# Summing four Mamba states per quarter on TensorE alone instead of halving them on VectorE first

## What is computed

```python
dA = jnp.exp(dt[..., None] * A)
dBx = dt[..., None] * Bm[:, :, None, :] * xs[..., None]
...
_, h = jax.lax.associative_scan(comb, (dA, dBx), axis=1)
y = jnp.einsum('blds,bls->bld', h, Cm) + D * xs
y = y * jax.nn.silu(z)
```

## Time and profile before

| | |
|---|---|
| median of 3 runs | 10564.35 us (10559.11 to 10570.2) |
| the profiled execution | 10562.82 us |
| its span, first to last instruction | 10560.5 us |
| PE matmul, busy | 71% |
| DVE, busy | 72% |
| ACT, busy | 56% |
| mean granted TensorE clock | 0.832 |

### The profile page before, as it was taken

One profiled execution on the slowest core, in us unless ns is written; L12 is line 12 of the kernel. 1 busy time (PEld: TensorE's weight loads), 2 busy tenths in 40 slices (PEclk: granted clock), 3 DMA queues, 4 the chain that ended last, 5 costly groups with the idle time before them and its releaser, 6 DMA issues. The chain is left out here.

```text
span 10560.5 us, 133751 instructions
## 1 busy us (share of the span) xinstructions
PE 7453.7 (71%) x40708; PEld 4281.7 (41%) x40708; DVE 7621.4 (72%) x10135; ACT 5890.6 (56%) x12843; POOL 796.9 (8%) x657
## 2 busy tenths in 40 slices
PE   6766666677777777777777777777777777777442
PEld 3434334444444444444444444444444444444221
DVE  3777777777777777777778777877777777777625
ACT  5555545556655665556555655565556555655211
POOL 0131313100000000000000000000000000000173
PEclk8878788888888888888888888888888888888655
DMA  3222222222222222222222222222222222222334
GB/s 125 92 84 85 92 77 100 84 94 104 95 91 94 104 98 91 91 104 102 88 91 107 100 91 92 102 99 91 99 95 100 97 95 93 105 91 86 102 60 124
DMA packets 284018, 1007.89 MB, mean 95 GB/s; under 512 B 45448, under 2 KB 135404, under 8 KB 275052
## 3 DMA queue, kind: packets, MB, share of 16 engines
q1 hardware_dynamic: 248556, 981.23, 25.7%
q0 software_dynamic: 34816, 21.19, 1.4%
HBM read 938.66 MB, written 63.58 MB: 95 GB/s over the span
## 5 line engine op out<-in xcount | busy, mean ns | idle before, releaser
L588 ACT ACTIVATE P<-psS,least_s 99x197 f32<-99x197 f32 x4096 | 1443.5, 432 | 1252.2 <-DVE least_s L759 1250.6
L1029 PE MATMUL psS<-KM,Q 128*99 128x394 f32 x4096 | 1952.3, 622 | 108.7 <-ACT PTs L594 105.7
L1036 PE MATMUL psS<-cst,P 99*99 99x99 f32 x8192 | 1227.2, 295 | 1071.2 <-ACT P L588 1048.5
L843 DVE TENSOR_TENSOR_SCAN hs<-dA,hs 128x1576 f32<-128x1576 f32 x512 | 1762.1, 3442 | 62.2
L1036 PEld LDWEIGHTS psS<-cst,P 99*99 99x99 f32 x8192 | 1034.7, 199 | 1590.8 <-ACT P L588 1383.1
L759 DVE TENSOR_REDUCE least_s<-psS 99x2 f32<-99x394 f32 x2048 | 1083.5, 561 | 611.1 <-PE psS L1029 586.2
L1029 PEld LDWEIGHTS psS<-KM,Q 128*99 128x99 f32 x4096 | 803.2, 212 | 966.4 <-issue 801.8
L664 ACT ACTIVATE dA<-dt_,aneg 128x394 f32<-128x394 f32 x2048 | 1160.9, 625 | 34.8 <-DVE hs L843 34.8
L594 ACT ACTIVATE PTs<-psS 99x396 f32<-99x396 f32 x2048 | 936.0, 531 | 430.5 <-PE psS L1036 428.8
L1119 PE MATMUL psY<-hs,cst 128*128 128x394 f32 x2048 | 897.9, 566 | 266.4 <-DVE hs L852 266.4
L834 DVE TENSOR_TENSOR hs<-hs,u 128x1576 f32<-128x1576 f32 x512 | 917.2, 1791 | 0.7 <-DMA hs<-bc_scratch 0.7
(11 more groups left out here) (186 smaller groups left out, 9778.3 us busy)
## 6 DMA issues: line engine op xcount, KB each, us to landing
hs<-bc_scratch SPq DMA_DIRECT2D x512, 788.0 KB, 4.1
cr<-bc_scratch SPq DMA_DIRECT2D x512, 788.0 KB, 5.6
pat<-patches SPq DMA_DIRECT2D x64, 1176.0 KB, 5.9
rows_scratch<-zeros SPq DMA_DIRECT2D x1, 19104.0 KB, 62.4
hs<-sum_scratch SPq DMA_DIRECT2D x24, 512.0 KB, 3.5
out<-hs SPq DMA_DIRECT2D x24, 512.0 KB, 2.6
sum_scratch<-HW SPq DMA_DIRECT2D x64, 148.5 KB
bc_scratch<-dtbc SPq DMA_DIRECT2D x128, 49.2 KB, 5.8
```

The source lines that it names most:

```text
L588: last = nc.scalar.activation(P[:, r, b, m, 0:T], psS[0:CT, 2 * r + b, m * T:(m + 1) * T], ACT.Exp, bias=least_s[:, r, b, m:m + 1], scale= ...
L843: nc.vector.tensor_tensor_scan(h, dA[:, g % 2, :, :].rearrange("p n t -> p (n t)"), h, 0.0, ALU.mult, ALU.add).then_inc(scan_ready, 1)
L1029: mm(psS[0:CT, 2 * r + b, 0:2 * T].rearrange("p (e t) -> p e t", e=2), Q[:, r, b, q * CT:(q + 1) * CT], KM[:, r, 2 * h:2 * h + 2, b, 0:T], ...
L1036: last = nc.tensor.transpose(psS[0:CT, 2 * r + b, at:at + CT], P[:, r, b, m, k * CT:(k + 1) * CT], c("ident")[0:CT, 0:CT])
```

## The change

`half` and its semaphore are gone, and PE's `sum_` waits for `mul_done` of the same quarter and issues four identity products in place of two. `UNITS` loses its eight `half` entries, and each list of `PLACE` the eight numbers that belonged to them. All other numbers stay.

```diff
@@ UNITS @@
-    UNITS += [("scan", _g)] + ([("half", _g - 1), ("sum", _g - 1)] if _g else [])
+    UNITS += [("scan", _g)] + ([("sum", _g - 1)] if _g else [])
...
-UNITS += [("half", QUARTERS - 1)]
@@ block.vector @@
-            def half(i, g):
-                dve.wait_ge(mul_done, i * MULS + MUL_OUT[g])
-                nc.vector.tensor_tensor(hs[:, g % HBUF, 0:2, :], hs[:, g % HBUF, 0:2, :], hs[:, g % HBUF, 2:4, :], ALU.add).then_inc(half_summed, 1)
@@ block.tensor, sum_ @@
-                pe.wait_ge(half_summed, i * QUARTERS + g + 1)
-                for k in range(2):
+                pe.wait_ge(mul_done, i * MULS + MUL_OUT[g])
+                for k in range(QN):
                     last = mm(psY[:, 0:N], c("ident"), hs[:, g % HBUF, k, :], start=q == 0 and k == 0, stop=False)
```

More of the change, by code:

```diff
@@ L82 @@
 STAGES = [('conv', 0), ('square', 1, 0), ('square', 0, 0), ('norm', 1, 0), ('norm', 0, 0), ('qkv', 1), ('qkv', 0), ('keys', 1, 0), ('keys', 0, 0), ('score', 1, 0, 0), ('score', 0, 0, 0), ('score', 1, 0, 1), ('score', 0, 0, 1), ('keys', 1, 1), ('keys', 0, 1), ('turn', 1, 0, 0), ('turn', 0, 0, 0), ('turn', 1, 0, 1), ('turn', 0, 0, 1), ('score', 1, 1, 0), ('score', 0, 1, 0), ('score', 1, 1, 1), ('score', 0, 1, 1), ('keys', 1, 2), ('keys', 0, 2), ('turn', 1, 1, 0), ('turn', 0, 1, 0), ('turn', 1, 1, 1), ('turn', 0, 1, 1), ('score', 1, 2, 0), ('score', 0, 2, 0), ('score', 1, 2, 1), ('score', 0, 2, 1), ('keys', 1, 3), ('turn', 1, 2, 0), ('keys', 0, 3), ('turn', 0, 2, 0), ('turn', 1, 2, 1), ('turn', 0, 2, 1), ('score', 1, 3, 0), ('score', 0, 3, 0), ('score', 1, 3, 1), ('score', 0, 3, 1), ('turn', 1, 3, 0), ('turn', 0, 3, 0), ('turn', 0, 3, 1), ('turn', 1, 3, 1), ('score', 1, 4, 0), ('score', 0, 4, 0), ('score', 1, 4, 1), ('value', 1, 0), ('score', 0, 4, 1), ('value', 0, 0), ('turn', 0, 4, 0), ('turn', 1, 4, 0), ('turn', 1, 4, 1), ('turn', 0, 4, 1), ('score', 1, 5, 0), ('score', 0, 5, 0), ('score', 1, 5, 1), ('score', 0, 5, 1), ('turn', 1, 5, 0), ('turn', 0, 5, 0), ('turn', 1, 5, 1), ('turn', 0, 5, 1), ('score', 1, 6, 0), ('score', 0, 6, 0), ('score', 1, 6, 1), ('score', 0, 6, 1), ('turn', 1, 6, 0), ('turn', 0, 6, 0), ('turn', 0, 6, 1), ('turn', 1, 6, 1), ('score', 0, 7, 0), ('score', 1, 7, 0), ('score', 1, 7, 1), ('score', 0, 7, 1), ('turn', 1, 7, 0), ('turn', 1, 7, 1), ('turn', 0, 7, 0), ('turn', 0, 7, 1), ('value', 1, 1), ('value', 0, 1), ('den', 1), ('den', 0), ('wo', 1), ('wo', 0), ('square', 1, 1), ('norm', 1, 1), ('square', 0, 1), ('norm', 0, 1), ('gate', 1), ('gate', 0), ('sig', 1), ('sig', 0), ('up', 1), ('up', 0), ('down', 1), ('down', 0), ('square', 1, 2), ('norm', 1, 2)]
-PLACE = {'dve': [0, 0, 0, 1, 3, 1, 2, 5, 8, 14, 14, 14, 15, 15, 16, 17, 19, 22, 25, 27, 27, 27, 28, 29, 30, 30, 32, 36, 38, 40, 40, 40, 41, 41, 45, 41, 42, 43, 43, 45, 47, 48, 49, 49, 49, 50, 51, 52, 52, 54, 55, 56, 57, 57, 51, 55, 59, 61, 63, 63, 64, 65, 66, 66, 66, 64, 68, 69, 72, 72, 75, 74, 75, 75, 75, 76, 77, 77, 78, 81, 82, 82, 86, 87, 89, 83, 84, 86, 88, 93, 90, 90, 90, 91, 91, 90, 92, 93, 97, 94, 95, 96, 98, 98, 99, 100], 'act': [0, 0, 0, 1, 3, 10, 5, 5, 8, 14, 11, 14, 15, 15, 16, 17, 19, 22, 25, 27, 27, 27, 28, 29, 30, 30, 32, 36, 38, 40, 40, 40, 41, 47, 47, 47, 47, 43, 43, 45, 47, 48, 49, 49, 49, 50, 51, 52, 51, 54, 55, 56, 57, 57, 57, 52, 59, 61, 63, 63, 64, 65, 66, 66, 66, 64, 68, 69, 72, 72, 72, 74, 79, 79, 79, 76, 77, 78, 80, 81, 79, 82, 82, 82, 84, 83, 84, 86, 88, 93, 87, 90, 90, 91, 91, 91, 92, 93, 94, 91, 95, 96, 98, 98, 99, 100], 'pe': [0, 0, 0, 1, 3, 4, 5, 5, 8, 14, 11, 14, 15, 15, 16, 17, 19, 22, 25, 27, 27, 27, 28, 29, 30, 30, 32, 36, 38, 40, 40, 40, 41, 41, 41, 41, 42, 43, 43, 45, 47, 48, 49, 49, 49, 50, 51, 52, 51, 58, 55, 56, 57, 57, 51, 52, 59, 61, 63, 63, 64, 65, 66, 66, 66, 64, 68, 69, 78, 78, 81, 80, 81, 81, 81, 82, 77, 78, 80, 84, 85, 82, 88, 89, 89, 83, 84, 86, 88, 93, 90, 90, 90, 91, 91, 91, 92, 93, 97, 95, 95, 96, 98, 98, 99, 100]}
@@ new lines @@
+PLACE = {'dve': [0, 0, 0, 1, 3, 1, 2, 5, 8, 14, 14, 14, 15, 15, 16, 17, 19, 22, 25, 27, 27, 27, 28, 29, 30, 30, 32, 36, 38, 40, 40, 40, 41, 41, 45, 41, 42, 43, 43, 45, 47, 48, 49, 49, 49, 50, 51, 52, 54, 55, 56, 57, 57, 51, 55, 59, 61, 63, 64, 65, 66, 66, 66, 64, 68, 69, 72, 75, 74, 75, 75, 75, 76, 77, 77, 81, 82, 82, 86, 87, 89, 83, 84, 86, 93, 90, 90, 90, 91, 91, 90, 92, 97, 94, 95, 96, 98, 99], 'act': [0, 0, 0, 1, 3, 10, 5, 5, 8, 14, 11, 14, 15, 15, 16, 17, 19, 22, 25, 27, 27, 27, 28, 29, 30, 30, 32, 36, 38, 40, 40, 40, 41, 47, 47, 47, 47, 43, 43, 45, 47, 48, 49, 49, 49, 50, 51, 52, 54, 55, 56, 57, 57, 57, 52, 59, 61, 63, 64, 65, 66, 66, 66, 64, 68, 69, 72, 72, 74, 79, 79, 79, 76, 77, 78, 81, 79, 82, 82, 82, 84, 83, 84, 86, 93, 87, 90, 90, 91, 91, 91, 92, 94, 91, 95, 96, 98, 99], 'pe': [0, 0, 0, 1, 3, 4, 5, 5, 8, 14, 11, 14, 15, 15, 16, 17, 19, 22, 25, 27, 27, 27, 28, 29, 30, 30, 32, 36, 38, 40, 40, 40, 41, 41, 41, 41, 42, 43, 43, 45, 47, 48, 49, 49, 49, 50, 51, 52, 58, 55, 56, 57, 57, 51, 52, 59, 61, 63, 64, 65, 66, 66, 66, 64, 68, 69, 78, 81, 80, 81, 81, 81, 82, 77, 78, 84, 85, 82, 88, 89, 89, 83, 84, 86, 93, 90, 90, 90, 91, 91, 91, 92, 97, 95, 95, 96, 98, 99]}
@@ L242, in vit_mamba_moe @@
         names = ("open_ready loaded patches_loaded pool_ready unused_ready rows_zeroed rows_stored init_stored hw_ready "
-                 "routed_stored q_waited ht_ready hw_free conv_done sent_all pair_free all_added fin_ready mul_done half_summed "
+                 "routed_stored q_waited ht_ready hw_free conv_done sent_all pair_free all_added fin_ready mul_done "
                  "slot_ready pool_waited sent_a sent_b slots_free e_out added act_setup consts_ready act_back xz_done xc_ready "
@@ L252, in vit_mamba_moe @@
          hw_ready, routed_stored, q_waited, ht_ready, hw_free, conv_done, sent_all, pair_free, all_added, fin_ready,
-         mul_done, half_summed, slot_ready, pool_waited, sent_a, sent_b, slots_free, e_out, added, act_setup,
+         mul_done, slot_ready, pool_waited, sent_a, sent_b, slots_free, e_out, added, act_setup,
          consts_ready, act_back, xz_done, xc_ready, xconv_ready, sge_ready, sg1_ready, sgr_ready, bc_done, dtbc_ready,
@@ L950, in _ @@
                  {"conv": conv, "sigmoid": sigmoid, "gate": gate, "dt": step_size, "input": input_, "scan": scan, "output": output,
-                  "half": half, "ys": ys, "merge": merge, "route": route_unit})
+                  "ys": ys, "merge": merge, "route": route_unit})
             assert (back.count[0], routing.count[0]) == (DVE_BACK, DVE_ROUTE), (back.count, routing.count)
```

## The result

The changed kernel takes **10690.33 us** (median of 4, 10687.81 to 10709.81), the kernel before 10566.13 in the same runs: a ratio of **1.0122** (95% 1.0105 to 1.014), slower by 1.2%. The profiled execution took 10692.48 us with a span of 10690.2, which is 129.7 longer than before.

A forecast was written before the change was run, and what follows sets the result against it. The prediction took no engine as the bound: PE, DVE and ACT wait in turn. Plain steps were put at 0, routing steps at 20 us and the end at 8: 10562.8 - 20 - 8 = 10535 us, range 10440 to 10670.

The forecast's parts named there:

- S1 (+2.6): Quarter 1's sum on PE and the scores behind it: without the half's wait, 2.6 us gained per step, capped by DVE.
- lead: How much earlier than in the kernel before a place in the step is reached, carried from place to place.
- Does a lead accumulate?: Over all steps: the clock restores even lengths, so 0 from the fifty plain steps and 20 us from routing steps.
- S2 (-1.2): Quarter 2's sum, between PE's transposes: delays those behind it, costing 1.2 us per step (0 to -1.35).
- S3 and S4 at nothing: Sums of quarters 3 and 4 on PE: no cost, since PE waits behind them anyway, 5.06 us behind quarter 4's.
- Gate and up products (+1.5): PE's two 1.2 GHz stretches around quarter 4's sum: 1.5 us gained per step, about a third of 4.4.
- S5 to S7 (-2.4): Sums of quarters 5 to 7, PE's run at the step's end: 1.62 us wait saved, 3 x 1.35 added, -2.4.
- The sum: All terms of one plain step: 0.5 us gained, with ends at -4.9 and +4.7.
- Routing steps (-2.0 each): Steps that still route: each gains 2.8 us, of which 2.0 was taken, 20 us in all.
- The end (-8): Last step, where DVE alone sets the pace, with the other partial steps: 8 us shorter.
- PE becomes the bound: Rival: quarter 1's sum stays at 1.2 GHz, plain steps 2.1 us longer, 10658 us; chance 0.24.
- The lead is kept: Rival: more of PE's work at 2.4 GHz and nothing given back, 1.4 us per step, 10457 us; chance 0.27.

The follow-up runs named there:

- zero products: Changed kernel plus two zero-weight products per step in PE's 2.2 us wait, ahead of the scores in the round behind quarter 1's sum: 10571.91 us, ratio 1.0009.
- two-product run: Changed kernel with only two identity products per sum and no halves, leaving states 2 and 3 of every quarter out: 10448.18 us, ratio 0.9894.
- both fills: Kernel before, halves kept, plus two zero-weight products behind quarter 1's sum and four ahead of the second xproj product, per step: 10541.96 us, ratio 0.9984.
- S1 alone: Kernel with only quarter 1 summed directly by four products, the seven other quarters halved on DVE as before: 10568.07 us, ratio 1.0002.
- S2 forward: Changed kernel with quarter 2's sum moved ahead on PE into its 2.2 us wait (78 to 70): 10550.04 us, ratio 0.9987.
- S5 forward: Changed kernel with quarter 5's sum moved ahead on PE into its 3.7 us wait for DVE (97 to 93): 10386.16 us, ratio 0.9841; repeat 10406.19, 0.9853.
- S2 and S5 forward together: Changed kernel with the sums of quarters 2 and 5 both moved ahead into PE's waits: 10415.93 us, ratio 0.986.

## Why the prediction was wrong

**S1 (+2.6): right, both its parts a little low and the cap making up for it.** S1 has no wait ahead of it and runs at 1.00. The scores behind it start 2.60 us earlier, where I had 1.8, and are 0.99 shorter, where I had 0.9. I had capped their sum at 2.6 by DVE: its last minimum of this round ends 76.10 us into the step before and 73.13 after, so 3.0 of lead pass there.

```profile
4541.30 1.89 DVE L759 TENSOR_REDUCE least_s<-psS 99x2 f32<-99x394 f32 x3 [0.39 <-PE psS L1029]
...
4598.30 1.99 DVE L759 TENSOR_REDUCE least_s<-psS 99x2 f32<-99x394 f32 x4
```

**What follows S1: the step that failed.** I priced S1 to the start of the scores and then let the lead run on. The sentence "now PE goes on working there, so I take 2.4 GHz" is true of S1 alone: a round later PE waits for ACT, does little for 3.4 us, and the transposes and most of the scores behind that run at half clock. From +2.60 to -0.36 that is 3.0 us lost, 1.8 of them in these scores alone, and 0.24 of lead is left where S2 starts, for which I had all 2.6. With the zero products in the gap the lead is +2.18 at the end of the scores (82.25 - 80.07) and +2.31 where S2 starts. I should have asked of each gap behind a moved piece what the clock does after it. The two-product run and the zero-product run show it from both sides: the slow scores come without added work, and they go with it. The gate products behind S4 follow: reached 2.2 us earlier in the run with zero products, they take 5.76 us in place of 6.77.

**"Does a lead accumulate?": wrong in what I made of it.** I took the evenness of 150.18 as a sign that leads, and so losses too, return to nothing, and put the fifty steps at 0. They lose 2.3 each, 115 us. The evenness is real, and stronger than I thought: five different kernels (before, before with both fills, S1 alone, S2 forward, zero products) have all or most of their steps at 150.19. But it is no law. Others settle at 160.42, or in patterns of two to seven steps. So the evenness of one kernel was no ground for putting the loss of another at 0. That the clock restores the step is consistent with these runs, but only argued; what sets the lengths stays open.

**S2 (-1.2): right.** From +0.24 where S2 starts (83.82 against 84.06) to -1.08 behind it, 1.3; in the run with zero products from +2.31 to +0.98, 1.3 too.

**S3 and S4 at nothing: right.** The lead is -1.08 behind S2 and -1.08 at the gate products behind S4. Quarter 5's load does show, as DVE's wait of 0.70, inside a wait that is there anyway.

**Gate and up products (+1.5): too high.** About nothing in two of the three kinds of step: the products behind S4 take 6.77 us (6.70 before), at half clock at first as in the earlier trace rows. In the third the products ahead of S4 run at full clock, and it ends 2.4 better than its neighbour (150.99 against 153.43): a mean of 0.8.

**S5 to S7 (-2.4): right.** From 34.09 to 36.25 us between the gate products and the copy, -2.2, and the run with S5 forward turns that to +1.65. (PE also waits 0.48 us at a norm in this part, in both kernels, so it is not quite as unbroken as I wrote.)

**The sum** is -3.24, -0.80 and -2.76 for the three kinds of step, -2.3 on average, where I had +0.5 and then took 0.

**Routing steps (-2.0 each): wrong in sign.** They take 172.6, 1.9 longer. I had read one place of them alone, S6; where they lose was not taken apart. **The end (-8): right,** 8.7.

**The rivals.** "PE becomes the bound" gave 10658, the nearest. Its size was by chance: its condition, S1 at 1.2 GHz and ending late, did not occur. "The lead is kept" failed at the same round as my forecast. My test for telling them, the clock at S1, pointed at 1.00 and so to the faster rival, while the kernel was slower.

**What stays open:** why two zero products help the changed kernel by 118 us the one with S1 alone by about 0.2%, and the one with S5 forward not at all, though the scores behind them run at full clock in all three; why S2 and S5 forward together do not add up; and the patterns' lengths.

## What to carry to other kernels

In a kernel like this one, where PE waits often, a 1.2 GHz stretch behind a wait can be part of the price of an edit: after moving a piece, follow PE to the next gap that it leaves, and work out the forecast with what runs behind that gap at half clock as well. Try added products where PE waits, not in its unbroken run; here one sum moved into a wait was worth 2.7 to 2.8% of the changed kernel, and even products with zero weights paid for themselves there, though not in every version. Price the whole step and not one round: full clock in one round gave next to nothing in two of these runs. And do not judge an edit with only its own placement: with PE's waits filled, the same change turned from 1.2% slower to 1.3% faster.

## What the hardware showed that I had not expected

Steps of quite different kernels lock to one length, 150.19 us, most of them to within 0.02. Other kernels repeat patterns over two, three, four, six or seven steps, as 153.43, 150.99 and 152.95 here, with no difference in the instructions of the steps. Adding 128 zero-weight products (two in each of 64 steps) took 118 us off. On another chip the routing steps, with their indirect DMAs, took 181 to 192 us, where they took 170.67 in the kernel before and 164 to 178 in all kernels traced elsewhere; no one kernel was traced on both.
